# A perceiver layer on one core: chunks of 128 + 128 + 1 keys with the last key's products stacked, and layer norm vectors loaded as rows

## The chip, the cores and the metric

The kernel runs on one core of a Trainium2 chip. The core has a matrix engine (TensorE, PE in the rows), VectorE (DVE), ScalarE (ACT), GpSimd (POOL) and SyncE (SP), each with its own queue of instructions, and 16 DMA engines. The engines work side by side and wait for one another by semaphores. The metric is the device time of one execution in microseconds (us), as the median of several runs.

## The reference

Two layer norms, a cross attention over 257 keys for each of 32 batches, a self attention over 32 tokens, and a mixture of experts with two of eight experts for each token:

```python
x = x + xattn(layernorm(x), ctx, g_x, b_x, g_c, b_c, Wq, Wk, Wv, Wo)   # x (32, 32, 512), ctx (32, 257, 384)
x = x + attn(layernorm(x), W_qkv, W_o)
x = x + moe(layernorm(x), gate_w, gate_b, w1, b1, w2, b2, ln_g, ln_b)  # top 2 of 8, FF 2048

def xattn(x, context, ...):
    xn = layer_norm(x, g_x, b_x)
    cn = layer_norm(context, g_c, b_c)
    q, k, v = (heads(t) for t in (xn @ Wq, cn @ Wk, cn @ Wv))          # 16 heads of 64
    sim = einsum('bhid,bhjd->bhij', q, k) * 64 ** -0.5
    return merge(einsum('bhij,bhjd->bhid', softmax(sim), v)) @ Wo
```

## The kernel before

The 1024 tokens are eight groups of 128, and a group is four batches of 32 tokens. Groups 1 to 6 are one loop on each engine; groups 0 and 7 are written apart. The body of a group runs the cross attention of group g together with the self attention and the routing of group g - 1. After the groups comes the mixture of experts: 23 jobs of 128 rows, whose matmuls are lines 546 and 564.

The keys are not projected. The queries are carried through Wk into the 384 columns of the context (`qk_proj`, L1183), so the scores are products with the normalized context itself (`scores`, L1199), and so is the other side: `av` (L1240) multiplies the probabilities with the normalized context n. That product wants more than one half precision pass, so n and the probabilities p are each split into a high and a low half-precision part, and three products are summed in one PSUM bank: n_high·p_high, n_low·p_high and n_high·p_low.

The 257 keys of a batch stand on the partitions in three chunks, `PART = [86, 86, 85]` at `KOFF = [0, 86, 172]`. Each step per chunk is therefore done three times: the statistics of the context (`cn_stats`, L915 to L922), its normalization (`cn_apply`, L930), its high part (`n_hi`, ScalarE, L814) and low part (`n_lo`, VectorE, L969), the transposes of the context (`ct_fill`, L1208) and of the probabilities (`pt_fill`, L1222), the high part of those (`pt_hi`, ScalarE, L821), their low part (`pt_lo`, VectorE, L962), and the matmuls of `av`: three products of three chunks, nine for each 128 of the 384 columns (c = 0, 1, 2).

In a group, TensorE goes through steps b = 0 to 4. In step b stand the scores of batch b in four parts, with the transposes of the probabilities of batch b - 1 between (in step 0: the context transposes of batch 1), and then the three `av` of batch b - 1, in steps 1, 2 and 4 each with one `ct_fill` ahead for a batch to come. Step 1 also has the scores of the self attention (`ss_fill`, L1302), step 4 its product with the values (`pv_fill`, L1313). VectorE in step b reduces the scores of batch b, normalizes its probabilities (`norm_probs`, L955, for which `pt_fill` of step b + 1 waits), and normalizes a context ahead; in step 2 it also has `ss_sub` (L986, L987), after step 3 `ss_norm` (L993 to L999), for which `pv_fill` waits. The order on each engine is that of the code: `body` of each engine is written out by hand.

At the start, ScalarE loads the vectors g_x, b_x, g_c, b_c into columns (L771 to L774): one element to a partition, 1792 elements of 4 bytes. They are the scale and bias of `xn_out` (L782) and `ct_out` (L789). SyncE loads x, the weights and the contexts; each context is two transfers (`ctx_load`): 255 rows to 85 partitions, and the last two rows to partition 85. A context of the next group is loaded as soon as the third `av` of the batch in the same slot is done.

## Time and profile before

| | |
|---|---|
| median of 3 runs | 1579.29 us (1573.94 to 1582.66) |
| the profiled execution's own time | 1575.59 us |
| its span (first to last instruction) | 1574.0 us |
| mean granted TensorE clock | 0.981 |
| PE busy | 1472.5 us, 94% of the span |
| VectorE busy | 679.8 us, 43% |
| ScalarE busy | 448.8 us, 29% |
| GpSimd busy | 114.0 us, 7% |
| DMA | 140.25 MB, mean 89 GB/s |
| starts of the query matmuls of groups 2 and 3 | 221.33 and 317.55 us, 96.2 apart |

The span has three parts: until 24 us TensorE has next to nothing to do; from there to 850 us run the eight groups and the end of the routing; the jobs of the experts take the rest. Matmuls are pipelined, and the busy time of one (its mean of 0.38 us, say) is longer than the distance to the next: what a matmul costs a full TensorE is read from the starts of the rows.

### The profile page before, as it was taken

The numbers are of one execution on the slowest core, as the hardware profiler recorded it, in microseconds if no ns is written. First come the engines' busy times: TensorE is split into PE (matmuls) and PEld (weight loads), VectorE is DVE, ScalarE is ACT, GpSimd is POOL, SyncE is SP. The second block draws the span as 40 slices with busy tenths as digits, with TensorE's granted clock in tenths as the row PEclk, the third lists the DMA queues.
The fourth block names the chain that finished last, engine by engine and source line by source line (L and its number), as shares of the span: only waits on it lengthen the run. The fifth ranks groups of instructions, "written<-read, shape, count | busy, mean of one in ns | idle before, by whom it ended". The sixth has DMA issues, their size and how long they took to land.

```text
span 1574.0 us, 22638 instructions
## 1 busy us (share of the span) xinstructions
PE 1472.5 (94%) x7708; PEld 913.7 (58%) x7709; DVE 679.8 (43%) x1822; ACT 448.8 (29%) x916; POOL 114.0 (7%) x167
## 2 busy tenths in 40 slices
PE   3899999999999999999965999999999999999997
PEld 3668686686866769677552444444444444444442
DVE  2764747657476674765533312112112212212215
ACT  1553626445263452625401111111111111111100
POOL 1000010000100101010011000000000000000005
PEclk9999999999999999999976999999999999999997
DMA  8680000000000010000056251606051346000005
GB/s 276 229 303 2 31 24 10 30 13 30 23 18 22 13 32 22 20 23 12 1 214 236 105 225 68 240 13 260 20 214 59 121 152 260 14 19 20 13 7 167
DMA packets 42784, 140.25 MB, mean 89 GB/s; under 512 B 4792, under 2 KB 4792, under 8 KB 37632
## 3 DMA queue, kind: packets, MB, share of 16 engines
q0 software_dynamic: 16256, 83.89, 14.0%
q1 hardware_dynamic: 24640, 55.93, 10.5%
q8 instruction: 20, 0.33, 0.1%
q10 hardware_dynamic: 1856, 0.01, 0.1%
q14 instruction: 12, 0.10, 0.0%
HBM read 110.46 MB, written 29.36 MB: 89 GB/s over the span
## 4 chain that ended last, share of the span: by engine, by line
PE 80%; DVE 11%; issue 3%; ACT 2%; DMA 2%; POOL 1%; ACTq 0%; SPq 0%; DVEq 0%; POOLq 0%
PE bank L546 20%; PE bank L564 20%; PE bank L1199 7%; PE bank L1240 6%; PE bank L1162 4%; PE bank L1265 4%; PE bank L1183 3%; PE bank L1253 3%; PE bank L556 3%; PE bank L1287 2%; PE bank L1321 2%; PE bank L1222 2%; DMA ccol<-in_L_xattn_b_c_dram 1%; DVE mx L945 1%; DVE cstats L915 1%
## 5 line engine op out<-in xcount | busy, mean ns | idle before, releaser
L546 PE MATMUL bank<-moe_w,arena 128*128 x736 | 332.4, 595 | 2.3 <-POOL pool_mark L354 2.3
L564 PE MATMUL bank<-moe_w,arena 128*128 x736 | 330.9, 592 | 0.0
L458 DVE TENSOR_TENSOR arena<-bank,arena 128x512 f32<-128x512 f32 x92 | 63.7, 692 | 478.5 <-PE bank L546 478.5
L546 PEld LDWEIGHTS bank<-moe_w,arena 128*128 128x128 f32 x736 | 140.3, 191 | 178.7 <-issue 178.7
L396 ACT ACTIVATE arena<-arena 128x512 f32<-128x512 f32 x92 | 57.9, 630 | 578.6 <-DVE arena L458 578.6
L564 PEld LDWEIGHTS bank<-moe_w,arena 128*128 128x128 f32 x736 | 132.7, 190 | 132.5 <-issue 132.5
L1199 PE MATMUL bank<-moe_w 128*128 128x257 f32 x768 | 188.4, 382 | 2.4 <-DVE moe_w L765 2.4
L1240 PE MATMUL bank<-moe_w 86*128 86x512 f16 (+1 forms) x576 | 153.4, 379 | 5.1 <-ACT moe_w L821 3.3
L1199 PEld LDWEIGHTS bank<-moe_w 128*128 128x128 f32 x768 | 137.2, 190 | 21.8 <-DVE moe_w L765 2.6
L807 ACT ACTIVATE moe_w<-bank,ccol,ugain 128x512 f32<-128x512 f32 x96 | 74.6, 778 | 92.8 <-PE bank L1240 91.9
L962 DVE TENSOR_TENSOR moe_w<-bank,moe_w 86x512 f16<-86x512 f32 (+1 forms) x96 | 64.5, 685 | 69.7 <-ACT moe_w L821 69.5
L1240 PEld LDWEIGHTS bank<-moe_w 86*128 86x128 f16 (+1 forms) x576 | 54.0, 97 | 57.9 <-ACT moe_w L821 4.3
L1240 PE MATMUL bank<-moe_w,arena 86*128 86x512 f16 (+1 forms) x288 | 78.0, 379 | 0.0
L1162 PE MATMUL bank<-arena,moe_w 128*128 128x128 f32 x512 | 60.8, 281 | 13.4 <-ACT arena L782 13.4
L821 ACT CAST moe_w<-bank 86x512 f16<-86x512 f32 (+1 forms) x96 | 53.4, 580 | 54.6 <-PE bank L1222 54.6
L1162 PEld LDWEIGHTS bank<-arena,moe_w 128*128 128x128 f32 x512 | 59.7, 197 | 13.8 <-issue 13.8
L1222 PE MATMUL bank<-ident,moe_w 128*86 128x128 f32 (+1 forms) x384 | 55.5, 274 | 12.3 <-DVE moe_w L955 10.9
L556 PEld LDWEIGHTS bank<-ident,arena 128*128 128x128 f32 x368 | 45.3, 141 | 36.9 <-issue 36.9
L465 DVE COPY arena<-bank 128x512 f32<-128x512 f32 x92 | 62.9, 684 | 4.5 <-PE bank L556 2.9
L800 ACT ACTIVATE moe_w<-bank,negm 128x257 f32<-128x257 f32 x128 | 59.9, 473 | 10.0 <-DVE negm L947 9.5
L692 POOL TENSOR_TENSOR crstd<-cmv,half 86x3 f32<-86x3 f32 x32 | 30.1, 939 | 438.2 <-DVE cmv L922 438.2
L765 DVE COPY moe_w<-bank 128x512 f32<-128x512 f32 x48 | 33.1, 691 | 65.7 <-PE bank L1183 65.7
(188 smaller groups left out, 1595.4 us busy)
## 6 DMA issues: line engine op xcount, KB each, us to landing
moe_w<-in_L_ffn_w_dram POOLq DMA_DIRECT2D x16, 4096.0 KB, 19.4
xs_rows<-blocks SPq DMA_DIRECT2D x8, 2048.0 KB, 13.8
arena<-in_ctx_dram SPq DMA_DIRECT2D x32, 382.5 KB
arena<-in_L_ffn_b_dram POOLq DMA_DIRECT2D x8, 1024.0 KB, 26.7
arena<-xs_rows SPq DMA_DIRECT2D x23, 256.0 KB, 2.7
ys_rows<-arena SPq DMA_DIRECT2D x23, 256.0 KB, 2.0
moe_w<-in_L_xattn_Wq_dram SPq DMA_DIRECT2D x1, 2048.0 KB, 9.7
moe_w<-in_L_xattn_Wo_dram SPq DMA_DIRECT2D x1, 2048.0 KB, 21.8
```

What stands on the lines that cost most here:

```text
L458: nc.vector.tensor_tensor(h_sb[:, fb % 2, :], bank[fb % 2][:, :], b1_rows[:, bass.ds(slot * FF + fb * 512, 512)], ALU.add).then_inc(h_bias ...
L465: nc.vector.tensor_copy(hT_sb[:, fb % 2, :, :].rearrange("p c t -> p (c t)"), bank[2 + fb % 2][:, :]).then_inc(hT_out, 1)
L546: last = nc.tensor.matmul(bank[fb % 2][:, :], xsT[:, k, :], moe_flat[:, bass.ds((e % 2) * 16384 + k * FF + fb * 512, 512)], start=(k == 0) ...
L556: last = nc.tensor.transpose(bank[2 + fb % 2][:, c * P:(c + 1) * P], h_sb[:, fb % 2, c * P:(c + 1) * P], ident[:, :])
L564: last = nc.tensor.matmul(Y[:, :], hT_sb[:, fb % 2, c, :], moe_flat[:, bass.ds((e % 2) * 16384 + 8192 + (4 * fb + c) * DIM, DIM)], start=( ...
L807: nc.scalar.activation(uT[:, c, b, :, :], M[at % 2][:, :].rearrange("p (h t) -> p h t", t=TOK), ACT.Identity, bias=ccol[:, 1, c:c + 1], sc ...
L962: nc.vector.tensor_tensor(pT_low[0:PART[k], k, :], src[0:PART[k], :], pT_high[0:PART[k], k, :], ALU.subtract).then_inc(emptied, 1)
L1162: last = nc.tensor.matmul(ps[:, m * P:(m + 1) * P], wq[:, k, (4 * i + m) * P:(4 * i + m + 1) * P], xnT[:, k, :], start=(k == 0), stop=(k = ...
L1199: last = nc.tensor.matmul(bank[h][:, 0:KEYS], qkT[:, c, b, h * P:(h + 1) * P], cnT[:, b % 2, c, :], start=(c == 0), stop=(c == KC - 1))
L1222: last = nc.tensor.transpose(into[0:PART[k], h * P:(h + 1) * P], probs[:, h, KOFF[k]:KOFF[k] + PART[k]], ident[:, :])
L1240: last = nc.tensor.matmul(ps[:, :], n_part[0:PART[k], k, c * P:(c + 1) * P], p_part[0:PART[k], k, :], start=(k == 0 and i == 0), stop=(k = ...
L1265: last = nc.tensor.matmul(ps[:, 0:256], oT[:, m, :], wo[:, m, j * 256:(j + 1) * 256], start=(m == 0), stop=(m == KI - 1))
```

## The change

`PART` becomes [128, 128, 65] and `KOFF` [0, 128, 256]. The first 256 keys fill two chunks of 128 partitions. The last key stands three times in a third chunk of 65 partitions, in partitions 0, 32 and 64 (`LAST_AT`); the partitions between hold zeros, written once by GpSimd before the first context is loaded. For the last key the three products of `av` are stacked on those three partitions: partition 0 has n_high and p_high, partition 32 n_low and p_high (n_lo writes its third chunk there, into `n_high`), partition 64 n_high and p_low (pt_lo writes there, into `pT_high`). One matmul of 65 partitions sums the three, so `av` has 2 + 2 + 2 + 1 matmuls. The third transposes of the probabilities read the one column of the last key, broadcast to 65. A context is loaded by four transfers: 256 rows to 128 partitions, and the last row to each of three partitions.

The layer norm vectors are loaded as 14 rows of 128 elements into a free part of `y2`; one TensorE transpose turns them, ScalarE copies the 14 columns, and `gcol` and `ccol` are views of the copy.

```diff
@@ -46,8 +46,9 @@
 KI = INNER // P
 KF = FF // P
 HG = HEADS // GB
-PART = [86, 86, 85]
-KOFF = [0, 86, 172]
+PART = [P, P, 65]
+KOFF = [0, P, 2 * P]
+LAST_AT = (0, 32, 64)
 ZERO_FIRST = 3
 FB = FF // 512
 JOBS = TOKENS * TOPK // P + EXPERTS - 1
@@ -148,8 +149,10 @@
         before = sb("before", [P, P])
         ones = sb("ones", [P, P])
         gate = sb("gate", [P, KD, EXPERTS])
-        gcol = sb("gcol", [P, 2, KD])
-        ccol = sb("ccol", [P, 2, KC])
+        cols = sb("cols", [P, 2 * KD + 2 * KC])
+        gcol = cols[:, 0:2 * KD].rearrange("p (k c) -> p k c", k=2)
+        ccol = cols[:, 2 * KD:2 * KD + 2 * KC].rearrange("p (k c) -> p k c", k=2)
+        col_rows = y2[0:2 * KD + 2 * KC, 0:P]
         ugain = sb("ugain", [P, KC])
         gate_bias = sb("gate_bias", [P, EXPERTS])
         half = sb("half", [P, 8])
@@ -240,6 +243,7 @@
         x0_in = sem("x0_in")
         x_in, wk_in, wq_in, wv_in, wo_in = sem("x_in"), sem("wk_in"), sem("wq_in"), sem("wv_in"), sem("wo_in")
         qkv_in, wos_in, cols_in, rows_in, gate_in = sem("qkv_in"), sem("wos_in"), sem("cols_in"), sem("rows_in"), sem("gate_in")
+        cols_full, cols_ok = sem("cols_full"), sem("cols_ok")
         ctx_in = [sem(f"ctx_in{b}") for b in range(GB)]
         xs_zeroed = sem("xs_zeroed")
         consts, ident_ok, zeros_ok, memset_ok = sem("consts"), sem("ident_ok"), sem("zeros_ok"), sem("memset_ok")
@@ -251,7 +255,7 @@
         m_full, m_free = sem("m_full"), [sem(f"m_free{i}") for i in range(2)]
         qk_full, qk_out = sem("qk_full"), [sem(f"qk_out{i}") for i in range(2)]
         pt3_full, pt3_out = sem("pt3_full"), sem("pt3_out")
-        n_high_done, n_low_done, p_high_done, ugain_ok = sem("n_high_done"), sem("n_low_done"), sem("p_high_done"), sem("ugain_ok")
+        spare_zero, n_high_done, n_low_done, p_high_done, ugain_ok = sem("spare_zero"), sem("n_high_done"), sem("n_low_done"), sem("p_high_done"), sem("ugain_ok")
         b_full, b_free = sem("b_full"), sem("b_free")
         s_full, max_done, neg_done, exp_done = sem("s_full"), sem("max_done"), sem("neg_done"), sem("exp_done")
         rinv_done, norm_done = sem("rinv_done"), sem("norm_done")
@@ -617,10 +621,10 @@
         def ctx_load(sp, g, b):
 
             row = (g * GB + b) * KEYS
-            sp.dma_start(ctx[0:85, b, :, :].rearrange("p k c -> p (k c)"),
-                         ctx_rows[bass.ds(row, 255), :].rearrange("(p k) c -> p (k c)", k=3)).then_inc(ctx_in[b], 16)
-            sp.dma_start(ctx[85:86, b, 0:2, :].rearrange("p k c -> p (k c)"),
-                         ctx_rows[bass.ds(row + 255, 2), :].rearrange("(p k) c -> p (k c)", k=2)).then_inc(ctx_in[b], 16)
+            sp.dma_start(ctx[:, b, 0:2, :].rearrange("p k c -> p (k c)"),
+                         ctx_rows[bass.ds(row, 2 * P), :].rearrange("(p k) c -> p (k c)", k=2)).then_inc(ctx_in[b], 16)
+            for p in LAST_AT:
+                sp.dma_start(ctx[p:p + 1, b, 2, :], ctx_rows[bass.ds(row + 2 * P, 1), :]).then_inc(ctx_in[b], 16)
 
         @block.sync
         def _(sp):
@@ -632,6 +636,7 @@
 
             sp.dma_start(x_all[:, 0, :], x_rows[0:P, :]).then_inc(x0_in, 16)
             sp.dma_start(wq, Wq.rearrange("(c p) n -> p c n", p=P)).then_inc(wq_in, 16)
+            sp.wait_ge(spare_zero, 1)
             ctx_load(sp, 0, 0)
             sp.dma_start(wk_rows, Wk.rearrange("(c p) n -> p c n", p=P)).then_inc(wk_in, 16)
             sp.dma_start(qkv_rows, W_qkv.rearrange("(c p) n -> p c n", p=P)).then_inc(qkv_in, 16)
@@ -664,6 +669,7 @@
         def _(pool):
             nc.gpsimd.memset(ones[:, :], 1.0).then_inc(memset_ok, 1)
             nc.gpsimd.memset(half[:, :], -0.5).then_inc(memset_ok, 1)
+            nc.gpsimd.memset(ctx[:, :, 2, :], 0.0).then_inc(spare_zero, 1)
             pool.wait_ge(memset_ok, 2)
             nc.gpsimd.affine_select(out=ident[:, :], in_=ones[:, :], compare_op=ALU.is_equal, fill=0.0, base=0,
                                     pattern=[[-1, P]], channel_multiplier=1).then_inc(ident_ok, 1)
@@ -689,7 +695,7 @@
             def cn_pow(n):
 
                 pool.wait_ge(cn_var, n + 1)
-                nc.gpsimd.tensor_tensor(crstd[0:86, :], cmv[0:86, :, 1], half[0:86, 0:3], ALU.pow).then_inc(cn_rstd, 1)
+                nc.gpsimd.tensor_tensor(crstd[:, :], cmv[:, :, 1], half[:, 0:3], ALU.pow).then_inc(cn_rstd, 1)
 
             def body(g, do_a, do_b, nxt):
                 ln = ln_before(g)
@@ -767,12 +773,13 @@
 
         @block.scalar
         def _(act):
-            with nc.allow_non_contiguous_dma(reason="a few columns"):
-                act.dma_start(gcol[:, 0, :], g_x.rearrange("(c p) -> p c", p=P)).then_inc(cols_in, 16)
-                act.dma_start(gcol[:, 1, :], b_x.rearrange("(c p) -> p c", p=P)).then_inc(cols_in, 16)
-                act.dma_start(ccol[:, 0, :], g_c.rearrange("(c p) -> p c", p=P)).then_inc(cols_in, 16)
-                act.dma_start(ccol[:, 1, :], b_c.rearrange("(c p) -> p c", p=P)).then_inc(cols_in, 16)
-            act.wait_ge(cols_in, 64)
+            act.dma_start(col_rows[0:KD, :], g_x.rearrange("(c p) -> c p", p=P)).then_inc(cols_in, 16)
+            act.dma_start(col_rows[KD:2 * KD, :], b_x.rearrange("(c p) -> c p", p=P)).then_inc(cols_in, 16)
+            act.dma_start(col_rows[2 * KD:2 * KD + KC, :], g_c.rearrange("(c p) -> c p", p=P)).then_inc(cols_in, 16)
+            act.dma_start(col_rows[2 * KD + KC:, :], b_c.rearrange("(c p) -> c p", p=P)).then_inc(cols_in, 16)
+            act.wait_ge(cols_full, 1)
+            nc.scalar.copy(cols[:, :], BK[:, 0:2 * KD + 2 * KC]).then_inc(cols_ok, 1)
+            act.wait_ge(cols_ok, 1)
             nc.scalar.activation(ugain[:, :], ccol[:, 0, :], ACT.Identity, scale=1.0 / (N_SCALE * P_SCALE)).then_inc(ugain_ok, 1)
 
             def xn_out(n):
@@ -910,7 +917,7 @@
             def cn_stats(g, b):
 
                 bt, slot = GB * g + b, b % GB
-                dve.wait_ge(ctx_in[slot], 32 * (g + b // GB + 1))
+                dve.wait_ge(ctx_in[slot], 64 * (g + b // GB + 1))
                 for k in range(3):
                     last = nc.vector.bn_stats(cstats[0:PART[k], k, :], ctx[0:PART[k], slot, k, :])
                 link = chain(dve, cn_step, 2 * bt)
@@ -919,7 +926,7 @@
                 for k in range(3):
                     last = nc.vector.bn_aggr(cmv[0:PART[k], k, :], cstats[0:PART[k], k, :])
                 link(last)
-                nc.vector.tensor_scalar(cmv[0:86, :, 1], cmv[0:86, :, 1], EPS, None, ALU.add).then_inc(cn_var, 1)
+                nc.vector.tensor_scalar(cmv[:, :, 1], cmv[:, :, 1], EPS, None, ALU.add).then_inc(cn_var, 1)
 
             def cn_apply(g, b):
 
@@ -959,16 +966,16 @@
 
                 dve.wait_ge(p_high_done, 3 * (GB * g + b) + k + 1)
                 src, _, _, emptied = pt_place(g, b, k)
-                nc.vector.tensor_tensor(pT_low[0:PART[k], k, :], src[0:PART[k], :], pT_high[0:PART[k], k, :],
-                                        ALU.subtract).then_inc(emptied, 1)
+                rows, low = (slice(0, P), pT_low[:, k, :]) if k < 2 else (slice(64, 65), pT_high[64:65, 2, :])
+                nc.vector.tensor_tensor(low, src[rows, :], pT_high[rows, k, :], ALU.subtract).then_inc(emptied, 1)
 
             def n_lo(g, b):
 
                 dve.wait_ge(n_high_done, GB * g + b + 1)
                 for k in range(3):
-                    last = nc.vector.scalar_tensor_tensor(out=n_low[0:PART[k], b, k, :], in0=ctx[0:PART[k], b, k, :],
-                                                          scalar=N_SCALE, in1=n_high[0:PART[k], b % 2, k, :],
-                                                          op0=ALU.mult, op1=ALU.subtract)
+                    rows, low = (slice(0, P), n_low[:, b, k, :]) if k < 2 else (slice(32, 33), n_high[32:33, b % 2, 2, :])
+                    last = nc.vector.scalar_tensor_tensor(out=low, in0=ctx[rows, b, k, :], scalar=N_SCALE,
+                                                          in1=n_high[rows, b % 2, k, :], op0=ALU.mult, op1=ALU.subtract)
                 last.then_inc(n_low_done, 1)
 
             def heads_apart(g):
@@ -1219,7 +1226,8 @@
                 if k == 0:
                     pe.wait_ge(norm_done, GB * g + b + 1)
                 for h in range(HG):
-                    last = nc.tensor.transpose(into[0:PART[k], h * P:(h + 1) * P], probs[:, h, KOFF[k]:KOFF[k] + PART[k]], ident[:, :])
+                    part = probs[:, h, KOFF[k]:KOFF[k] + P] if k < 2 else probs[:, h, 2 * P:KEYS].to_broadcast([P, PART[2]])
+                    last = nc.tensor.transpose(into[0:PART[k], h * P:(h + 1) * P], part, ident[:, :])
                 last.then_inc(full, 1)
 
             def av(g, b, c):
@@ -1236,9 +1244,10 @@
                             pe.wait_ge(tp_free, tp(g, ("pt", b, 2)) + 1)
                         else:
                             pe.wait_ge(pt3_out, 2 * (g + 1))
-                    for k in range(3):
-                        last = nc.tensor.matmul(ps[:, :], n_part[0:PART[k], k, c * P:(c + 1) * P], p_part[0:PART[k], k, :],
-                                                start=(k == 0 and i == 0), stop=(k == 2 and i == 2))
+                    for k in range(2):
+                        nc.tensor.matmul(ps[:, :], n_part[:, k, c * P:(c + 1) * P], p_part[:, k, :], start=(k == 0 and i == 0), stop=False)
+                last = nc.tensor.matmul(ps[:, :], n_high[0:PART[2], b % 2, 2, c * P:(c + 1) * P], pT_high[0:PART[2], 2, :],
+                                        start=False, stop=True)
                 last.then_inc(m_full, 1)
 
             def o_proj(g, i):
@@ -1400,6 +1409,8 @@
                     rk_fill(g - 1)
 
             pe.wait_ge(ident_ok, 1)
+            pe.wait_ge(cols_in, 64)
+            nc.tensor.transpose(BK[:, 0:2 * KD + 2 * KC], col_rows, ident[0:2 * KD + 2 * KC, 0:2 * KD + 2 * KC]).then_inc(cols_full, 1)
             xn_fill(0, 2)
             pe.wait_ge(wq_in, 16)
             body(0, True, False, True)
```

The order of the instructions. First, TensorE in group 0, step 1: the last scores, and the first `ct_fill` and `av` (L1199, L1208 and L1240 before are L1206, L1215, and L1248 with L1249 now). A matmul of 32-bit data stands once here and twice in the trace. Before:

```order
L1199 MATMUL bank<-moe_w 128x257 x3
L1208 MATMUL bank<-ident,arena 128x86 x2
L1208 MATMUL bank<-ident,arena 128x85
L1240 MATMUL bank<-moe_w 128x512 x3
L1240 MATMUL bank<-moe_w,arena 128x512 x3
L1240 MATMUL bank<-moe_w 128x512 x3
```

With the change:

```order
L1206 MATMUL bank<-moe_w 128x257 x3
L1215 MATMUL bank<-ident,arena 128x128 x2
L1215 MATMUL bank<-ident,arena 128x65
L1248 MATMUL bank<-moe_w 128x512 x2
L1248 MATMUL bank<-moe_w,arena 128x512 x2
L1248 MATMUL bank<-moe_w 128x512 x2
L1249 MATMUL bank<-moe_w 128x512
```

Two of nine matmuls of 512 columns are gone, and the context transposes have 321 columns in place of 257. Next, the queue of ScalarE at the start; before:

```order
L771 DMA gcol<-in_L_xattn_g_x_dram 128x4x1
L772 DMA gcol<-in_L_xattn_b_x_dram 128x4x1
L773 DMA ccol<-in_L_xattn_g_c_dram 128x3x1
L774 DMA ccol<-in_L_xattn_b_c_dram 128x3x1
L776 ACT_TABLE_LOAD
L776 ACTIVATE ugain<-ccol 128x3 [waits cols_in]
L782 ACTIVATE arena<-bank,gcol 128x128 [waits tp_full]
```

With the change:

```order
L776 DMA arena<-in_L_xattn_g_x_dram 4x128
L777 DMA arena<-in_L_xattn_b_x_dram 4x128
L778 DMA arena<-in_L_xattn_g_c_dram 3x128
L779 DMA arena<-in_L_xattn_b_c_dram 3x128
L781 ACT_TABLE_LOAD
L781 COPY cols<-bank 128x14 [waits cols_full]
L783 ACTIVATE ugain<-cols 128x3 [waits cols_ok]
L789 ACTIVATE arena<-bank,cols 128x128 [waits tp_full]
```

The wait for the four transfers moves from ScalarE to TensorE, whose new first instruction (L1413) waits for them and for `ident`. Last, the queue of SyncE at the start; before:

```order
L634 DMA moe_w<-in_L_xattn_Wq_dram 128x4x1024
L620 DMA arena<-in_ctx_dram 85x1152
L622 DMA arena<-in_ctx_dram 1x768
L636 DMA moe_w<-in_L_xattn_Wk_dram 128x3x1024
L637 DMA moe_w<-in_L_attn_W_qkv_dram 128x4x512
```

With the change:

```order
L638 DMA moe_w<-in_L_xattn_Wq_dram 128x4x1024
L624 DMA arena<-in_ctx_dram 128x768
L627 DMA arena<-in_ctx_dram 1x384 x3
L641 DMA moe_w<-in_L_xattn_Wk_dram 128x3x1024
L642 DMA moe_w<-in_L_attn_W_qkv_dram 128x4x512
```

Each context has two more transfers to issue, and the first one now waits for GpSimd's zeros.

## Rows read from the trace of the kernel before

**Rows 1.** Windows: length, busy time of each engine, clock, DMA share, GB/s.

```profile
317.00:413.00 96.00, 92.28 (x708) 69.89 (x708) 62.80 (x188) 43.22 (x96) 8.41 (x12) 1.00 0.07 22
...
36.00:40.00 4.00, 2.53 (x24) 2.26 (x23) 1.03 (x3) 2.59 (x5) 0.00 (x0) 1.00 1.06 308
...
48.00:56.00 8.00, 7.18 (x66) 6.69 (x65) 4.77 (x12) 4.15 (x8) 0.55 (x1) 0.79 1.04 390
```

**Rows 2.** Timeline of the start: start, us, engine, line, tile [idle before].

```profile
2.23 1.79 POOL L682 MEMSET arena<- 128x2048 f32 x1
...
2.57 0.86 ACTq L774 DMA_DIRECT2D ccol<-in_L_xattn_b_c_dram  x1
...
9.55 1.09 PE L1273 MATMUL bank<-ident,arena 128*128 128x128 f32 x4 [9.55 <-DVE arena L900]
...
22.32 0.20 ACT L776 ACTIVATE ugain<-ccol 128x3 f32<-128x3 f32 x1 [17.58 <-DMA ccol<-in_L_xattn_b_c_dram]
...
24.07 9.19 PE L1162 MATMUL bank<-arena,moe_w 128*128 128x128 f32 x64 [13.43 <-ACT arena L782]
...
38.30 3.66 PE L1142 MATMUL bank<-ident,moe_w 128*128 128x128 f32 x32
...
47.06 5.47 PE L1183 MATMUL bank<-moe_w 64*128 64x128 f32 x64 [2.32 <-DVE moe_w L765]
```

**Rows 3.** Timelines of the start and of group 3: issues on SyncE's queue.

```profile
1.40 0.42 SPq L634 DMA_DIRECT2D moe_w<-in_L_xattn_Wq_dram  x1
...
4.17 4.00 SPq L638 DMA_DIRECT2D moe_w<-in_L_attn_W_o_dram  x1
...
358.55 0.26 SPq L620 DMA_DIRECT2D arena<-in_ctx_dram  x1
```

**Rows 4.** DMA issues: transfers, KB, median us from issue to landing.

```profile
moe_w<-in_L_xattn_Wq_dram SPq DMA_DIRECT2D x1, 2048.0 KB, 9.7
...
moe_w<-in_L_attn_W_o_dram SPq DMA_DIRECT2D x1, 1024.0 KB, 21.9
...
gcol<-in_L_xattn_b_x_dram ACTq DMA_DIRECT2D x1, 2.0 KB, 14.2
```

**Rows 5.** Timeline of TensorE in group 3.

```profile
350.72 0.81 PE L1240 MATMUL bank<-moe_w 86*128 86x512 f16 x3
...
352.67 0.39 PE L1208 MATMUL bank<-ident,arena 86*128 86x86 f32 x3
...
352.90 0.81 PE L1240 MATMUL bank<-moe_w 86*128 86x512 f16 x3
...
376.44 0.60 PE L1222 MATMUL bank<-ident,moe_w 128*85 128x128 f32 x4
...
384.27 1.51 PE L1222 MATMUL bank<-ident,moe_w 128*86 128x128 f32 x12
...
386.55 0.82 PE L1240 MATMUL bank<-moe_w 86*128 86x512 f16 x3 [0.55 <-ACT moe_w L821]
...
392.08 1.08 PE L1313 MATMUL bank<-blocks,v_sb 128*32 128x128 f32 x32 [1.22 <-DVE blocks L999]
```

**Rows 6.** Timeline of VectorE in group 3.

```profile
360.91 0.69 DVE L962 TENSOR_TENSOR moe_w<-bank,moe_w 86x512 f16<-86x512 f32 x1 [3.73 <-ACT moe_w L821]
...
367.32 1.47 DVE L915 BATCH_NORM_STATS2 cstats<-arena 86x6 f32<-86x384 f32 x3
...
375.51 0.69 DVE L962 TENSOR_TENSOR moe_w<-bank,moe_w 86x512 f16<-86x512 f32 x1 [2.40 <-ACT moe_w L821]
...
383.07 1.14 DVE L955 TENSOR_SCALAR moe_w<-moe_w,rinv 128x257 f32<-128x257 f32 x4
```

**Rows 7.** Timeline of ScalarE in group 3.

```profile
366.50 0.56 ACT L789 ACTIVATE moe_w<-bank,ccol 128x257 f32<-128x257 f32 x1
```

**Rows 8.** Timeline of VectorE in group 7.

```profile
759.67 0.69 DVE L962 TENSOR_TENSOR moe_w<-bank,moe_w 86x512 f16<-86x512 f32 x1 [4.87 <-ACT moe_w L821]
```

**Rows 9.** Waits of the first 135 us: total, times, longest.

```profile
DVE cstats L915 <- DMA arena<-in_ctx_dram: 12.6, 2, 7.0
```

## Prediction

> **What bounds the kernel now.** I read the windows first, for the share of TensorE by stage, then the timelines of TensorE, VectorE and ScalarE over one group beside one another, for which wait ends last, then the start, then the DMA issues. In group 3, as in every group of the loop, TensorE is busy 92.28 of 96 us at the full clock of 2.4 GHz [rows 1]. So a removed matmul could be worth its whole length, but only where no other engine stands right behind. Before 24.07 TensorE has only four transposes: ScalarE waits 17.58 us for the last of the column loads, and the query matmuls wait for ScalarE [rows 2]. The experts are untouched.
>
> **The start.** The column loads were issued by 3.4 us; the last lands at 22.3, and 1.75 us later the query matmuls begin (22.32 to 24.07) [rows 2]. That these loads are slow for their number of pieces and not their size I take from 2 KB that need 14.2 us [rows 4]. The new ones are 14 rows of 512 bytes. I take them to land before the transposes of x are done, at 9.55 + 1.09 = 10.64 [rows 2]. Then the next thing late is either Wq, issued at 1.40 and landed 9.7 later, at 11.1 [rows 3, 4], or ScalarE's part, 10.64 + 1.65 = 12.3 (the 1.75 without the 0.1 of `ugain`). So the query matmuls start at 12.3 in place of 24.07: -11.8. The new transpose and copy of 14 columns lie ahead of 10.64 and cost nothing; if the rows landed only at 14, each us behind 10.6 would be one less gained.
>
> GpSimd's zeros are 1,536 elements a partition; 2,048 take 1.79 [rows 2], so 1.34. That delays `ident` to about 3, unseen, and SyncE's first context by under 1 us, while the DMA engines still have Wq to do. Of the six extra issues of the first contexts each may hold the queue for a while. What is late next are the weights: the transposes of W_qkv and W_o would run at 38.30 - 11.8 = 26.5 [rows 2], and W_o lands at 4.17 + 21.9 = 26.1 [rows 3, 4]. That is no wait by 0.4. Bounds for the start: -8 (the weights land some 4 us later, through the extra issues) to -12.5 (ScalarE's 1.65 hidden in part).
>
> **Price of a matmul and a transpose.** From 350.72 to 352.67 stand the nine matmuls of an `av` (the row's three, three times): 1.95, so 0.217 each, and an `av` becomes 7 x 0.217 = 1.52, 0.43 less. From 352.67 to 352.90 a `ct_fill` takes 0.23 for 257 columns [rows 5]; for 321 by columns 0.29, +0.06. (Twelve transposes of 128 columns take 1.51 [rows 5], 0.126 each at most, which bounds it at +0.15.) Over 96 `av` that would be -41.7, over 96 `ct_fill` +5.8. ScalarE and VectorE have as many instructions of the same free size as before; rows of 85 and 86 partitions took the same in every group of the trace, so I take 0 for 128, 65 and 1. The broadcast weight load of 65 columns lies beside a matmul; I take 0, between -0.02 and +0.05 for each of 128.
>
> **A loop group, step by step** (times of before; in brackets the shift so far).
> - Step 0: three `ct_fill`, then VectorE's chain behind the last scores: [+0.18].
> - Step 1: three `av` save 1.30, three `ct_fill` cost 0.18. The second `ct_fill` must now wait for ScalarE's `ct_out`, which stands behind four exponentials (the same place in step 2: 366.50 + 0.56 [rows 7]): +0.2. VectorE has slack, since it sits idle 3.73 before 360.91 [rows 6]. [-0.8].
> - Step 2: the `av` get shorter, but the transposes at 376.44 [rows 5] wait for VectorE's instruction at 375.51 + 0.69 = 376.20 [rows 6], which by its chain (n_lo, statistics, norm_probs, apply, ss_sub, then ScalarE's exponential, n_hi, pt_hi) starts from step 2's last probabilities and not from an `av`. The slack is 0.1. [-0.9].
> - Step 3: `norm_probs` ends at 383.07 + 1.14 = 384.21, and the transposes that wait for it start at 384.27 [rows 5, 6]. No slack, and VectorE's own shift is still that of step 1: 1.3 saved turns into a wait. [-0.8].
> - Step 4: the first two `av` come before `pv_fill`, which already waits 1.22 for VectorE [rows 5]. Their 0.86 goes into that wait. The third saves 0.43, a `ct_fill` costs 0.06. [-1.2].
>
> So -1.2 in each of six groups: -7.2, of the 6 x (12 x 0.43 - 12 x 0.06) = 27 that the matmuls and transposes themselves give there. Bounds: -0.6 (the transposes at 0.15, more waits of step 1's kind) to -2.5.
>
> **Group 7** has no contexts ahead in steps 2 to 4. VectorE sits idle 4.87 in step 3 [rows 8], so steps 2 and 3 keep theirs: 0.18 - 1.0 - 0.9 - 1.3 - 0.4 = -3.5 (-2 to -4.5). **Group 0** has no `ss_sub`, so step 2 keeps 0.9: 0.18 - 0.9 - 0.9 and nothing in steps 3 and 4, in which VectorE waits for a context behind the filling of the expert rows (two waits on contexts, 12.6 in all, 7.0 of them at the start, so 5.6 here [rows 9]): -1.9 (-3 to +1, since all of it now comes 12 us closer to the same transfers).
>
> **The clock.** The changed groups leave TensorE idle 2.2 us ahead of `pv_fill` (1.22 + 0.86 and a little) and 1.6 us ahead of the transposes of step 4. In the trace an idle 2.32 before 47.06 [rows 2] was followed by a fall to 1.2 GHz: the window from 48 to 56 has a granted clock of 0.79, so 8 x 0.21 = 1.7 us lost [rows 1]. The shorter wait ahead of step 1's first transposes is in every loop group, at a full clock. I take one fall in the whole kernel, +1.7; bounds 0 to 7 x 1.7 = 12. The Trainium skill says in "TensorE: Matmul & The Clock Gate" (Part 4, PE-mode transpose) that transposes do not count as activity for the clock. By that rule the transposes and the waits ahead of and behind them in step 4 are one gap. Here 32 transposes followed others from 38.30 on, and the clock stayed at 1.00 [rows 1, 2], so the trace speaks against it. The gap would run from 382 to 386, 3.9 us, and cost a fall in each group; this is a rival below.
>
> **Sum.** -11.8 - 7.2 - 3.5 - 1.9 + 1.7 = -22.7. The profiled execution took 1575.6, so 1552.9; it lies 3.7 under the median of the runs, 1579.3, from which it would be 1556.6. Between the two I forecast 1554.
>
> **Rivals.**
> - *The clock falls once in each group* at `pv_fill` or by the gap of step 4: 12 in place of 1.7, 1564. For it: the one idle of this length in the groups was followed by a fall. Against it: that one had matmuls of 64 partitions only around it. 17%.
> - *It falls twice in each group*: 24, which takes all back: 1576, no change. 5%.
> - *The start gives little*, because rows or weights land late and the extra issues hold SyncE: half of it, 1560 to 1564. 10%.
> - *The removed matmuls count in full*: 1575.6 - 11.8 - 41.7 + 5.8 = 1528. For it: TensorE at 92.28 of 96. Against it: steps 2 to 4 above. 5%.
> - *The one-row transfers are slow*: a context is issued at 358.55 [rows 3], read at 367.32 [rows 6], 8.8 later. If a transfer of one row took the 14.2 of the 2 KB load [rows 4], VectorE would wait 5.4 in step 2, where there is no slack, in at least seven groups: 1553 + 38 = 1591 or more, slower. It decides from 8.8 us on. Against it: a transfer to one partition is part of each load now, and the loop shows no wait for it. 3%.
> - That the change does less than it says I see no room for: the matmuls are gone from the program. 2% for what I have not seen.
>
> **Chances.** My case 58%. A measurement of this kernel tells a change from none at about 0.5%, 7.9 us; faster by more are my case and all rivals but the twofold fall, the slow rows and part of the unseen: 0.91; within 0.5%: 0.06; slower: 0.03. The range holds my case with the bounds of its terms, and the first and third rival: 1545 to 1566; my case alone is 1547 to 1560.
>
> **What would show it.** Start: the first query matmul near 12.3, waiting for ScalarE, and the transposes of W_qkv without a wait. Loop: a period of 95.0 in place of 96.2; an `av` of 1.52 and a `ct_fill` of 0.29 by their starts; waits of some 1.6 and 2.2 us ahead of the transposes of step 4 (for VectorE's L955) and ahead of `pv_fill` (for its blocks), and about 0.8 at the third transposes of step 3. Wrong: a period under 94 (VectorE is no bound), a clock under 1.00 in a loop group, a wait for a context there, or a group 0 longer than before.

## The result, and the profile after

The changed kernel took 1566.57 us (median of 6 runs, 1562.93 to 1567.33), the kernel before 1579.3 us (1573.94 to 1582.66, 6 runs): a ratio of 0.9916, 95% interval 0.9901 to 0.9931. That is faster by 0.8%, by 12.7 us of the medians and by 9.0 us of the profiled spans (1574.0 to 1565.0). The forecast was 1554 with a range of 1545 to 1566: the direction was right, the gain too large by 10 to 14 us, and the time just outside the range.

By the starts of each group's query matmuls the two traces divide so:

| | before | after | difference | forecast |
|---|---|---|---|---|
| start of the query matmuls | 24.07 | 11.69 | -12.4 | -11.8 |
| group 0 | 101.15 | 99.5 | -1.6 | -1.9 |
| groups 1 to 6 | 6 x 96.2 | 585.2 | +8.0 | -7.2 and +1.7 for the clock |
| group 7 and the end of the routing | 148.3 | 145.2 | -3.1 | -3.5 |
| experts | 723.3 | 723.4 | +0.1 | 0 |

The start, from the timeline of TensorE and then of ScalarE after (it answers to [rows 2]):

```profile
7.03 0.25 PE L1413 MATMUL bank<-ident,arena 14*128 14x14 f32 x1 [7.03 <-DMA arena<-in_L_xattn_b_c_dram]
8.91 1.09 PE L1282 MATMUL bank<-ident,arena 128*128 128x128 f32 x4 [1.63 <-DVE arena L907]
11.69 9.36 PE L1169 MATMUL bank<-arena,moe_w 128*128 128x128 f32 x64 [1.69 <-ACT arena L789]
...
26.20 1.04 PE L1149 MATMUL bank<-ident,moe_w 128*128 128x128 f32 x8
```

```profile
10.04 1.51 ACT L789 ACTIVATE arena<-bank,cols 128x128 f32<-128x128 f32 x4 [2.31 <-PE bank L1282]
```

The fourteen rows are there at 7.03, ahead of the normed x. The transposes of the late weights (L1149) stand there without a wait, as forecast.

The loop did not get shorter. The three longest waits of TensorE in group 5 of the changed kernel (502 to 598 us): who waited for whom, total, times, longest.

```profile
PE bank L1230 <- DVE moe_w L962: 3.3, 2, 1.9
PE bank L1322 <- DVE blocks L1006: 2.1, 1, 2.1
PE bank L1230 <- DVE moe_w L970: 0.8, 1, 0.8
```

All three are for VectorE: L1230 are the transposes of the probabilities, L1322 is `pv_fill`. They are the waits that the prediction named: 1.9 ahead of the transposes of step 4 (forecast 1.6), 2.1 ahead of `pv_fill` (2.2) and 0.8 in step 3 (0.8); the other 1.4 of the first line was there before. Windows of the changed kernel (columns as in [rows 1]): groups 2 and 5; then group 2 during `pv_fill`, which follows the wait of 2.09, and in the four us behind it; then the transposes of step 4 in group 3.

```profile
209.00:307.00 98.00, 90.44 (x686) 68.64 (x685) 64.00 (x189) 43.08 (x96) 8.61 (x12) 0.98 0.07 22
...
502.00:598.00 96.00, 88.43 (x683) 67.76 (x683) 63.87 (x188) 43.08 (x96) 8.41 (x12) 1.00 0.07 22
284.00:285.00 1.00, 0.89 (x32) 0.84 (x32) 1.00 (x3) 0.00 (x0) 0.00 (x0) 1.00 0.00 0
285.00:289.00 4.00, 4.00 (x19) 1.85 (x12) 2.92 (x14) 1.41 (x3) 0.85 (x1) 0.57 0.01 2
374.00:378.00 4.00, 3.82 (x18) 3.21 (x19) 3.16 (x6) 2.28 (x4) 0.00 (x0) 0.57 0.17 69
```

TensorE's busy time in a group went from 92.28 [rows 1] to 88.43 where the clock stays up, 3.9 us less, and the group takes no less: 97.9, 98.0, 97.0, 97.9, 96.3 and 98.0 us for groups 1 to 6, against 96.2. VectorE, on which TensorE waits, has gone up from 62.80 [rows 1] to 63.87. In four groups the granted clock falls to the lower level (1.2 GHz) behind `pv_fill`, in a fifth at the transposes of step 4; only group 5 has none. The timelines of TensorE in groups 2 and 5 show what a fall costs:

```profile
284.11 1.08 PE L1322 MATMUL bank<-blocks,v_sb 128*32 128x128 f32 x32 [2.09 <-DVE blocks L1006]
...
285.46 1.02 PE L1248 MATMUL bank<-moe_w 128*128 128x512 f16 x2
286.27 1.06 PE L1248 MATMUL bank<-moe_w,arena 128*128 128x512 f16 x2
```

```profile
577.10 1.08 PE L1322 MATMUL bank<-blocks,v_sb 128*32 128x128 f32 x32 [2.09 <-DVE blocks L1006]
...
578.45 0.59 PE L1248 MATMUL bank<-moe_w 128*128 128x512 f16 x2
578.88 0.59 PE L1248 MATMUL bank<-moe_w,arena 128*128 128x512 f16 x2
```

Two f16 matmuls of 512 columns take 0.81 by their starts (285.46 to 286.27) instead of 0.43. A group with such a fall is 1.5 to 1.7 us longer than group 5, the one with the fall at step 4 0.7 (97.0). The wait is 2.09 in both cases, so its length alone does not decide.

Group 5 had no fall and was still 1.3 longer than the forecast of 95.0. VectorE in group 3 (timeline):

```profile
353.22 0.69 DVE L970 TENSOR_TENSOR moe_w<-bank,moe_w 1x512 f16<-1x512 f32 x1 [0.53 <-ACT moe_w L828]
353.94 0.42 DVE L952 TENSOR_REDUCE mx<-bank 128x1 f32<-128x257 f32 x1
...
355.03 1.01 DVE L977 SCALAR_TENSOR_TENSOR arena<-arena,moe_w 128x384 f16<-128x384 f32 x2
356.06 0.55 DVE L977 SCALAR_TENSOR_TENSOR moe_w<-arena,moe_w 1x384 f16<-1x384 f32 x1
356.64 1.48 DVE L922 BATCH_NORM_STATS2 cstats<-arena 128x6 f32<-128x384 f32 x3
...
364.85 0.69 DVE L970 TENSOR_TENSOR moe_w<-bank,moe_w 128x512 f16<-128x512 f32 x1 [2.40 <-ACT moe_w L828]
365.46 0.41 DVE L952 TENSOR_REDUCE mx<-bank 128x1 f32<-128x257 f32 x1
```

From the low part of 128 partitions to the next instruction are 0.61 us (364.85 to 365.46), from that of one partition 0.72 (353.22 to 353.94). The three low parts of a context take 1.61 (355.03 to 356.64). In the kernel before these were:

```profile
338.00 1.48 DVE L969 SCALAR_TENSOR_TENSOR arena<-arena,moe_w 86x384 f16<-86x384 f32 x3
339.40 0.41 DVE L945 TENSOR_REDUCE mx<-bank 128x1 f32<-128x257 f32 x1
```

that is, 1.40. The duration of each instruction is as before; what has grown is the distance to its neighbours: 0.1 from the probabilities' low part to the instruction behind it, and 0.2 for the context's.

In steps 3 and 4 the probabilities' instruction follows another one of VectorE without a wait for ScalarE, and there it also starts late itself. The three low parts of the probabilities in step 4, of the changed kernel (group 5) and of a kernel whose low parts all start on partition 0 (`low_scratch`, below; group 3), by VectorE's timelines:

```profile
570.33 2.01 DVE L970 TENSOR_TENSOR moe_w<-bank,moe_w 128x512 f16<-128x512 f32 x3 [0.20 <-ACT moe_w L828]
572.37 0.69 DVE L1000 TENSOR_REDUCE ssum<-sS 128x16 f32<-128x512 f32 x1
```

```profile
368.29 1.88 DVE L970 TENSOR_TENSOR moe_w<-bank,moe_w 128x512 f16<-128x512 f32 x3 [0.21 <-ACT moe_w L828]
370.09 0.67 DVE L1000 TENSOR_REDUCE ssum<-sS 128x16 f32<-128x512 f32 x1
```

That is 2.04 against 1.80. Not all of it reaches the path: laid beside each other instruction by instruction, the two groups show that the 0.2 of the first two contexts go into waits for TensorE and ScalarE, and that the probabilities' four (0.14, 0.12, 0.20, 0.24) and the last two contexts' (0.22, 0.23) add up to the 1.15 by which VectorE is late at `blocks`, and the group with it.

### The profile page after: what moved, and what is told of

It is laid out like the page before. It is cut to its first block, busy times and chain, and to the rows that moved or that the text cites. A ratio compares the mean times of both kernels' runs of the same rounds, so it can differ in the third digit from the quotient of the medians.

```text
span 1565.0 us, 22371 instructions
## 1 busy us (share of the span) xinstructions
PE 1449.6 (93%) x7517; PEld 901.9 (58%) x7518; DVE 689.5 (44%) x1822; ACT 448.3 (29%) x917; POOL 115.2 (7%) x168
## 4 chain that ended last, share of the span: by engine, by line
PE 79%; DVE 13%; issue 4%; ACT 2%; POOL 2%; DMA 1%; DVEq 0%; ACTq 0%; SPq 0%; POOLq 0%
PE bank L550 20%; PE bank L568 20%; PE bank L1206 8%; PE bank L1169 4%; PE bank L1274 4%; PE bank L1248 3%; PE bank L1190 3%; PE bank L1262 3%; PE bank L560 3%; PE bank L1296 2%; PE bank L1230 2%; PE bank L1330 2%; DVE mx L952 2%; DVE cstats L922 1%; PE bank L1215 1%
## 5 line engine op out<-in xcount | busy, mean ns | idle before, releaser
L1206 PE MATMUL bank<-moe_w 128*128 128x257 f32 x768 | 188.7, 383 | 2.4 <-DVE moe_w L771 2.4
L1206 PEld LDWEIGHTS bank<-moe_w 128*128 128x128 f32 x768 | 137.3, 190 | 21.6 <-DVE moe_w L771 2.6
L1248 PE MATMUL bank<-moe_w 128*128 128x512 f16 x384 | 117.7, 389 | 4.6 <-ACT moe_w L828 2.5
L814 ACT ACTIVATE moe_w<-bank,cols,ugain 128x512 f32<-128x512 f32 x96 | 74.5, 777 | 64.8 <-PE bank L1249 64.8
L970 DVE TENSOR_TENSOR moe_w<-bank,moe_w 128x512 f16<-128x512 f32 (+1 forms) x96 | 65.6, 690 | 58.2 <-ACT moe_w L828 57.5
L1230 PE MATMUL bank<-ident,moe_w 128*128 128x128 f32 (+1 forms) x384 | 57.2, 279 | 29.5 <-DVE moe_w L962 23.9
L828 ACT CAST moe_w<-bank 128x512 f16<-128x512 f32 (+1 forms) x96 | 53.7, 582 | 66.8 <-PE bank L1230 66.8
L1230 PEld LDWEIGHTS bank<-ident,moe_w 128*128 128x128 f32 (+1 forms) x384 | 45.8, 141 | 45.3 <-DVE moe_w L962 26.9
L796 ACT ACTIVATE moe_w<-bank,cols 128x257 f32<-128x257 f32 x96 | 54.2, 564 | 25.4 <-PE bank L1215 25.2
L698 POOL TENSOR_TENSOR crstd<-cmv,half 128x3 f32<-128x3 f32 x32 | 30.1, 940 | 425.8 <-DVE cmv L929 425.8
## 6 DMA issues: line engine op xcount, KB each, us to landing
xs_rows<-blocks SPq DMA_DIRECT2D x8, 2048.0 KB, 12.4
```

Source lines behind the costliest of these rows:

```text
L814: nc.scalar.activation(uT[:, c, b, :, :], M[at % 2][:, :].rearrange("p (h t) -> p h t", t=TOK), ACT.Identity, bias=ccol[:, 1, c:c + 1], sc ...
L970: nc.vector.tensor_tensor(low, src[rows, :], pT_high[rows, k, :], ALU.subtract).then_inc(emptied, 1)
L1206: last = nc.tensor.matmul(bank[h][:, 0:KEYS], qkT[:, c, b, h * P:(h + 1) * P], cnT[:, b % 2, c, :], start=(c == 0), stop=(c == KC - 1))
L1230: last = nc.tensor.transpose(into[0:PART[k], h * P:(h + 1) * P], part, ident[:, :])
L1248: nc.tensor.matmul(ps[:, :], n_part[:, k, c * P:(c + 1) * P], p_part[:, k, :], start=(k == 0 and i == 0), stop=False)
```

## The experiments

All were timed in five rounds beside the kernel before, whose median was 1576.8 to 1577.2 us there and 1579.3 beside the changed kernel, which was not timed again: so up to 2.5 us of a difference of medians to the changed kernel can be that, and the ratios are the safer comparison. Periods are the distances between the query matmuls of groups 1 to 7. Periods and falls are those of one profiled execution of each kernel; the others differ in span and mean clock, so their falls may differ too. The four of `from0` below, for example, have spans of 1551.3 (the profiled one) to 1557.2 us at mean clocks of 0.980 to 0.977.

**Which half gave the gain?** The kernel before with the layer norm rows alone (all four loads, the transpose and the copy):

```diff
-                act.dma_start(gcol[:, 0, :], g_x.rearrange("(c p) -> p c", p=P)).then_inc(cols_in, 16)
...
+            act.dma_start(col_rows[0:KD, :], g_x.rearrange("(c p) -> c p", p=P)).then_inc(cols_in, 16)
...
```

> The kernel before with the vectors loaded as rows and turned by one transpose, and the keys still in chunks of 86, 86 and 85. By the traces the query matmuls of group 0 start 12.4 us earlier in the changed kernel; if all of that belongs to this part and nothing gives it back, 1579 - 12.4 = 1567, with a loop group of 96.2 as before. If part of the start's gain came from the new context transfers, less than 10 us.

Measured: 1564.34 us, ratio 0.992 (0.9899 to 0.994), span 1561.3; query matmuls at 11.51, six periods of 96.2. The rows alone give all of the gain, 12.5 us against the kernel before beside them, where 12.4 were expected; on top of them the chunks gave nothing.

**The chunks alone**, with the four old column loads and without their transpose and copy:

```diff
-            act.dma_start(col_rows[0:KD, :], g_x.rearrange("(c p) -> c p", p=P)).then_inc(cols_in, 16)
...
+                act.dma_start(gcol[:, 0, :], g_x.rearrange("(c p) -> p c", p=P)).then_inc(cols_in, 16)
...
```

> The changed kernel with the old column loads: chunks of 128, 128 and 1, the last key stacked. Theory (clock and VectorE): a loop group is 96.3 us where the clock stays up and 98.0 where it falls after the wait ahead of the product of the self attention's probabilities and values, so the kernel is 2 to 5 us slower than before, 1581 to 1584. The prediction's sum for this part alone was -10.9, so 1568.

Measured: 1573.69 us, ratio 0.9981 (0.9968 to 0.9994), span 1571.4. This is neither the 1581 to 1584 of my theory nor the prediction's 1568. The periods are 96.2, 96.9, 98.0, 96.3, 98.0 and 97.0: falls of both kinds, in five groups; that of the first, at step 4, costs nothing, since the wait ahead of `pv_fill` is shorter by it (1.13). The start was 4.4 us earlier than before, which I had not seen coming; by ScalarE's timeline of this kernel the last of the old loads had landed at 17.92, where it was 22.32 before [rows 2]:

```profile
17.92 0.20 ACT L779 ACTIVATE ugain<-ccol 128x3 f32<-128x3 f32 x1 [13.51 <-DMA ccol<-in_L_xattn_b_c_dram]
```

So the same column loads took 4.4 us less in this execution than in that of the kernel before; whether the other transfers did that is not shown. The loop of this kernel lost 5.3 us against before, which the start and groups 0 and 7 gave back.

**Is it the clock?** Two 32-bit matmuls of 512 columns, whose result nobody reads, fill the wait ahead of `pv_fill`:

```diff
                         if do_b and b == GB and c == 1:
+                            if do_a:
+                                filler()
                             pv_fill(g - 1)
+                for k in range(2):
+                    nc.tensor.matmul(bank[1][:, :], ident[:, :], wq[:, k, 0:512], start=True, stop=True)
```

> The changed kernel with two more 32-bit matmuls of 512 columns (0.86 us each) into a free bank just ahead of that product, where TensorE waits 2.09 us for VectorE. They compute nothing that is used. If the fall of the clock to 1.2 GHz after this wait costs 1.7 us in five of six groups: a clock of 1.00 in every loop group, periods of 96.3, and 7 to 9 us less than the changed kernel, 1558 to 1560. If the fall comes from something else (the wait ahead of the last transposes, the load of the engine over a longer time), or costs nothing: 1566, or later by up to 12 if the matmuls end up on the path.

Measured: 1561.01 us, ratio 0.9897 (0.9878 to 0.9915); periods 97.0, 96.3, 96.8, 96.3, 96.3, 96.3. Timeline of TensorE in group 2, where the changed kernel had its fall:

```profile
279.89 1.88 PE L1235 MATMUL bank<-moe_w,ident 128*128 128x512 f32 x4
282.14 1.08 PE L1326 MATMUL bank<-blocks,v_sb 128*32 128x128 f32 x32 [0.37 <-DVE blocks L1006]
...
283.49 0.59 PE L1252 MATMUL bank<-moe_w 128*128 128x512 f16 x2
283.92 0.59 PE L1252 MATMUL bank<-moe_w,arena 128*128 128x512 f16 x2
```

The work lies in the wait (0.37 us are left of 2.09) and every fall behind `pv_fill` is gone: 5.6 us less for doing more, where 7 to 9 were expected. By the ratios it is 3 us, and their intervals overlap; what shows the clock as a cause is the same filling on the kernel with 32 partitions below, timed beside it. What is left are two groups of 96.8 and 97.0, falls at step 4 (0.71 of the clock from 370 to 374 us in the windows of group 3), and a fall-free group of 96.3, so that something else is a cause too.

**Is it VectorE's instructions on one partition?** Both are written on 65 partitions into scratch instead. This leaves the low parts of the last key out (its high product is summed three times):

```diff
-(slice(64, 65), pT_high[64:65, 2, :])
+(slice(0, 65), pT_low[0:65, 2, :])
-(slice(32, 33), n_high[32:33, b % 2, 2, :])
+(slice(0, 65), n_low[0:65, b, 2, :])
```

> The changed kernel, but VectorE's two instructions on the last key's chunk work on 65 partitions and write to the low parts' own tiles and not on one partition into the high parts' tiles. It leaves the low parts of the last key out (its high product is summed three times). If an instruction on one partition cannot lie over its neighbours as the others do: the next instruction starts 0.61 us after pt_lo's third and not 0.72, n_lo's three take 1.40 and not 1.61, VectorE's chain is 0.3 us shorter in each step, a group without a fall is 95.0 to 95.5, and the kernel 5 to 8 us shorter than the changed one. If those instructions cost the same on one partition: no change, 1566.

Measured: 1553.2 us, ratio 0.9846 (0.9825 to 0.9866); periods 96.7, 95.2, 95.2, 96.8, 95.2, 95.2. Timeline of VectorE:

```profile
333.22 0.69 DVE L970 TENSOR_TENSOR moe_w<-bank,moe_w 65x512 f16<-65x512 f32 x1 [0.53 <-ACT moe_w L828]
333.83 0.41 DVE L952 TENSOR_REDUCE mx<-bank 128x1 f32<-128x257 f32 x1
...
334.90 1.48 DVE L977 SCALAR_TENSOR_TENSOR arena<-arena,moe_w 128x384 f16<-128x384 f32 x3
336.30 1.47 DVE L922 BATCH_NORM_STATS2 cstats<-arena 128x6 f32<-128x384 f32 x3
```

The spacings are 0.61 and 1.40 again, and a group without a fall takes 95.2, nearly the forecast 95.0. So these eight instructions cost 1.1 us of every group. Against the changed kernel it is 13 us (11 by the ratios) and not the 5 to 8 expected; its profiled execution also had two falls instead of five. But "one partition" and "another start partition" had changed together.

**Few partitions, or their place?** The same products on 32 partitions each: the probabilities' low part from 32, the context's from 0.

```diff
-(slice(64, 65), pT_high[64:65, 2, :])
+(slice(32, 64), pT_high[32:64, 2, :])
-(slice(32, 33), n_high[32:33, b % 2, 2, :])
+(slice(0, 32), n_high[0:32, b % 2, 2, :])
```

> The changed kernel, with the same products stacked, but with the low part of the last key's probabilities written on partitions 32 to 63 (its product stands on 32) and the low part of its context row on partitions 0 to 31 (its product stands on 0); the high product is on partition 64. VectorE's two instructions so have 32 partitions instead of one, everything else is as in the changed kernel. Theory A (an instruction on one partition takes VectorE longer than one on many): the next instruction starts 0.61 us after the third low part of the probabilities (0.72 in the changed kernel) and 1.40 us after the three low parts of a context began (1.61); a group without a clock fall takes 95.2 us, one or two of six have a fall of 1.6: about 1553 us, as with scratch on 65 partitions. Rival B (what counts is that the instruction writes in place, or starts on another partition than 0): the spacings stay 0.72 for the probabilities, which start on 32, and at most the contexts' are repaired: 1559 to 1563. Rival C (it grows as the partitions get fewer, 32 is between): 1558 to 1562 with both spacings halfway.

Measured: 1560.85 us, ratio 0.9892 (0.9876 to 0.9908); periods 97.4, 95.9, 95.9, 97.5, 95.9, 95.9. My theory A fell and rival B came true, in time and in spacings. VectorE in group 3 (timeline):

```profile
335.90 0.68 DVE L970 TENSOR_TENSOR moe_w<-bank,moe_w 32x512 f16<-32x512 f32 x1 [0.53 <-ACT moe_w L828]
336.62 0.42 DVE L952 TENSOR_REDUCE mx<-bank 128x1 f32<-128x257 f32 x1
...
337.71 1.02 DVE L977 SCALAR_TENSOR_TENSOR arena<-arena,moe_w 128x384 f16<-128x384 f32 x2
338.64 0.54 DVE L977 SCALAR_TENSOR_TENSOR moe_w<-arena,moe_w 32x384 f16<-32x384 f32 x1
339.11 1.46 DVE L922 BATCH_NORM_STATS2 cstats<-arena 128x6 f32<-128x384 f32 x3
```

Thirty-two partitions from 32 on are followed by the same 0.72 as one partition was; thirty-two from 0 on need 0.47, and the three together 1.40.

**One partition, but the first:**

```diff
-(slice(64, 65), pT_high[64:65, 2, :])
+(slice(0, 1), pT_high[0:1, 2, :])
```

> The changed kernel with one edit: the low part of the last key's probabilities is written on partition 0 instead of 64 (its product then stands on 0, the high product on 64). It is still an instruction on one partition. Theory A' (VectorE loses time not where an instruction has few partitions, but where it starts on another partition than 0; the 32 partitions from 32 cost 0.71 us to the next instruction, those from 0 cost 0.47): the next instruction starts 0.61 us after this one, the context's low part, still on partition 32, keeps its 0.58 and the three together 1.61; a group without a fall takes 95.7 us, with falls in two to five of six: 1558 to 1563 us. Rival (one partition is slow wherever it is, and 32 from partition 32 are slow for another reason): 0.72 us as before, 96.3 a group, 1565 to 1567 us.

Measured: 1554.66 us, ratio 0.9854 (0.9835 to 0.9873); periods 97.1, then five of 95.6. Timeline of VectorE:

```profile
334.63 0.68 DVE L970 TENSOR_TENSOR moe_w<-bank,moe_w 1x512 f16<-1x512 f32 x1 [0.53 <-ACT moe_w L828]
335.24 0.40 DVE L952 TENSOR_REDUCE mx<-bank 128x1 f32<-128x257 f32 x1
```

One partition is no slower than 128 where it is partition 0: 0.61. The time is 3 us below my range, since only one group had a fall. Moving one slice from 64 to 0 goes with 12 us less (10 by the ratios). Of them the spacings explain 0.75 in each of six groups (96.3 to 95.6), some 4.5; most of the rest are falls that did not come in this execution, and why they did not is not shown.

**Both from partition 0, with the full result.** The high product needs a partition where neither factor is low, so the probabilities' instruction covers all 65 and a column of zeros and minus ones decides where the low part comes:

```diff
-                nc.vector.tensor_tensor(low, src[rows, :], pT_high[rows, k, :], ALU.subtract).then_inc(emptied, 1)
+                    nc.vector.scalar_tensor_tensor(out=high, in0=high, scalar=keep[0:PART[2], 0:1], in1=src[0:PART[2], :],
+                                                   op0=ALU.mult, op1=ALU.add).then_inc(emptied, 1)
```

> The changed kernel with both low parts of the last key written by instructions that start on partition 0, with the full result: the context's on partitions 0 to 31; the probabilities' on partitions 0 to 64, as the high part times a column (minus one on partitions 32 to 63, zero on the others) plus the whole value, so that partition 32 gets the low part and 0 and 64 the high one. Theory A': spacings of 0.61 and 1.40 us as with the scratch, a group without a fall takes 95.2 us, two of six have one: 1552 to 1555 us. Rival (an instruction with three sources here takes longer, or scratch on its own is what helped): 95.8 a group or more, 1558 to 1562 us.

Measured: 1555.21 us, ratio 0.9863 (0.9839 to 0.9887); periods 95.3 and five of 95.4, and no fall. The profiled execution is the fastest of the four; the slowest is 5.9 us longer at a lower mean clock, so it may well have had falls. The instruction itself is a little dearer: 0.66 to the next, by VectorE's timeline.

```profile
333.42 0.74 DVE L977 SCALAR_TENSOR_TENSOR moe_w<-moe_w,keep,bank 65x512 f16<-65x512 f16 x1 [0.53 <-ACT moe_w L829]
334.08 0.41 DVE L956 TENSOR_REDUCE mx<-bank 128x1 f32<-128x257 f32 x1
```

**The kernel with 32 partitions and the filled wait.** Its edit is the two diffs shown above, of the 32 partitions and of `filler`, together.

> As the kernel with 32 partitions, with two unused 32-bit matmuls of 512 columns ahead of the product with the values, in the wait of about 2 us. Theory A (the rest of the falls is from that wait): no fall in any group, 95.2 us each: 1551 to 1552 us. Rival (falls come from the wait ahead of step 4's transposes): one or two stay, 1553 to 1554 us. If the matmuls reach out of the wait: 1556 us or more.

Measured: 1556.19 us, ratio 0.9862 (0.9844 to 0.9881); all six periods 95.8 or 95.9. The filling took both falls away, and 4.7 us: the slowest execution with it (1557.64) is faster than the fastest without (1559.39). The 1551 to 1552 expected rested on 95.2 a group; the level of 95.8 is that of the probabilities' instruction from partition 32, and the filling does not reach out of the wait, of which 0.37 is left.

**VectorE's queue in another order**, on the kernel with 32 partitions. `norm_probs` of step 3 goes ahead of the statistics, their use behind `ss_norm`; ScalarE's exponential comes in step 3 instead of 2:

```diff
-                    if ahead:
+                    if ahead and b < 3:
                         cn_stats(g, b + 2)
                     if do_a:
                         norm_probs(g, b)
+                    if ahead and b == 3:
+                        cn_stats(g, b + 2)
...
                     ss_norm(g - 1)
                 if nxt:
+                    cn_apply(g, 5)
                     cn_stats(g, 6)
```

> As the kernel with 32 partitions, and a new order in step 3 and 4: VectorE scales the probabilities of context 3 before the statistics of the next group's second context (0.9 us of work moved behind it) and applies these statistics behind the softmax of the self attention; ScalarE's exponentials of the self attention come one step later. Theory A (the wait of 1.9 us ahead of step 4's transposes and that of 1.8 to 2.1 us ahead of the product with the values are VectorE's queue): both get shorter by about 1 us each or go, and so does every fall of the clock: a group takes 93.2 to 94.5 us, the whole 1540 to 1548 us. Rival (the time then is bounded by ScalarE or by VectorE's sum of work over the group, and the waits come back elsewhere): 95 us a group, 1550 to 1553.

Measured: 1554.77 us, ratio 0.9858 (0.984 to 0.9877), above both expected ranges (1540 to 1548, 1550 to 1553); periods 93.8, then five of 95.5 or 95.6. TensorE in group 3 of this kernel:

```profile
370.40 1.08 PE L1325 MATMUL bank<-blocks,v_sb 128*32 128x128 f32 x32 [2.09 <-DVE blocks L1006]
...
372.00 1.06 PE L1251 MATMUL bank<-moe_w 128*128 128x512 f16 x2
```

The order is worth about 2 us a group (93.8 without a fall, 95.9 with the old order), but the fall now came in five of six groups and took 1.8 of them back. The wait of 2.09 stayed, against theory A.

**The same order without the chunks** (the kernel before with the rows and this order):

> The kernel before with only the layer norm vectors as rows, and with the new order of VectorE's and ScalarE's steps 3 and 4 (the keys in chunks of 86, 86 and 85, nothing stacked). It tells whether the chunks are worth anything once VectorE's queue is out of the way. Theory A (the chunks take 1.2 us of TensorE's path off a group, which VectorE's waits took back): this one takes 95.0 to 95.7 us a group, 1557 to 1561 us, 8 us or more above the same order with the chunks. Rival (the chunks never stood on the path): equal to the same order with the chunks within 3 us.

Measured: 1568.66 us, ratio 0.9944 (0.9928 to 0.9959); periods 96.6 or 96.7, half a us more than with the old order. The expected 95.0 to 95.7 did not come. The one wait that is longer than with the old order, by TensorE's waits of group 3 (0.5 there):

```profile
PE bank L1247 <- ACT moe_w L825: 1.3, 1, 1.3
```

The waits for VectorE (1.4 and 1.2 us) are as long as with the old order, so there was nothing for the new one to shorten, and ScalarE's later exponential was only a cost. The kernel is 14 us above the same order with the chunks; 4 of these are what the order costs here. Against the best kernel without chunks, the rows alone with 1564.34, the chunks with this order are worth 10 us.

**All together:** both low parts from partition 0, the order, the filled wait.

> As the kernel with both low parts from partition 0, with the new order of VectorE's and ScalarE's steps 3 and 4 and with the two unused 32-bit matmuls ahead of the product with the values. The same order with the probabilities from partition 32 and no unused matmuls took 95.5 us a group, with a wait of 2.1 us ahead of that product and the clock at half speed behind it in every group. Theory A (the fall costs 1.6 us in each group, the start partition 0.6): 93.3 us a group, 1539 to 1544 us. Rival (the wait ahead of that product grows by what is saved elsewhere, since VectorE's queue is the bound of the step): 94.5 us or more, 1547 to 1552 us.

Measured: 1540.52 us (5 runs, 1539.12 to 1541.15), ratio 0.9761 (0.9742 to 0.9779), with the full result: the fastest, 26 us under the changed kernel (24 by the ratios) and as theory A had it. Periods 93.5, then five of 93.6. TensorE's waits in group 3:

```profile
PE bank L1241 <- DVE moe_w L966: 1.4, 1, 1.4
PE bank L1263 <- ACT moe_w L829: 1.2, 1, 1.2
...
PE bank L1337 <- DVE blocks L1014: 0.2, 1, 0.2
```

## Why the prediction was right in part and wrong in size

*The start* held: 11.69 for 12.3. The next thing late was ScalarE's part, TensorE did not wait for the weights, and the rows had landed by 7.0, far ahead of 10.6.

*The price of a matmul and a transpose* held: 1.52 for an `av` (367.39 to 368.91) and 0.28 for a `ct_fill` (379.02 to 379.30). So did the mechanism that most of it turns into waits for VectorE in steps 2 to 4; 27 us of matmuls went, and the fall-free group of the scratch kernel is 95.2 for the 95.0 forecast. TensorE's timeline in group 3 of the changed kernel:

```profile
367.39 0.59 PE L1248 MATMUL bank<-moe_w 128*128 128x512 f16 x2
...
368.91 0.59 PE L1248 MATMUL bank<-moe_w 128*128 128x512 f16 x2
...
379.02 0.44 PE L1215 MATMUL bank<-ident,arena 128*128 128x128 f32 x3
379.30 0.60 PE L1248 MATMUL bank<-moe_w 128*128 128x512 f16 x2
```

*"ScalarE and VectorE have as many instructions of the same free size [...] so I take 0 for 128, 65 and 1"* failed for VectorE. The term is +1.1 us a group, 0 taken: 6.6 us in groups 1 to 6, and 7.8 with the 0.2 a group by which even 95.2 missed. I had looked at how long an instruction is by its free size and not at whether it may overlap its neighbours. The new low parts start on partitions 64 and 32 and everything around them on 0. In the runs, partition 64 (one row), 32 (one row) and 32 (32 rows) each cost 0.1 us at the instruction behind, and 0 (one, 32 or 65 rows) nothing; with no wait ahead of it such an instruction also starts 0.1 late itself (the context's: 1.03 for the two before it, 0.93 in the kernel with 32 partitions). And since VectorE had no slack in steps 2 and 3, as the forecast itself said, it went on the path.

The Trainium skill states this in "VectorE: DVE Perf Modes", section "Two Vector instructions with no wait between them": an instruction whose input or output starts in another group of 32 partitions than the last one read or written in that memory is held until all earlier ones have finished; how many partitions it has does not come into it. Every spacing shown here agrees. The page gives no price; the 0.1 and 0.2 are these traces'. By that rule, looked up beforehand, the term would have had its sign.

*"I take one fall in the whole kernel, +1.7; bounds 0 to 7 x 1.7 = 12"* failed too: five came in the loop, 4 x 1.7 + 0.7 = 7.5 us. A clock under 1.00 in a loop group was one of the prediction's own signs of being wrong. The rival "the clock falls once in each group", 1564 at 17%, had the right mechanism for this part, but that its time comes so near is partly luck: it counted 12 us of falls where 7.5 came, and nothing for VectorE, which cost as much again. I had argued against it from where the one known fall stood; the row itself, 2.32 idle and a fall, was the better guide, though not a sure one (see below). Its variant by the Trainium skill's rule on transposes ("TensorE: Matmul & The Clock Gate", Part 4) did not hold as the cause: of six groups with the same transposes in step 4 only one fell there. Both misses, (7.5 - 1.7) + 7.8 = 13.6, are the gap between the forecast for groups 1 to 6, -5.5, and the +8.0 that came.

*Groups 0 and 7* have slips of addition in the forecast: its own terms give 0.18 - 0.9 - 0.9 = -1.6 and not -1.9, and -3.4 and not -3.5, so its sum would be -22.3 and not -22.7. Measured were -1.6 and -3.1.

**Open:** why a wait of 2.09 us is followed by a fall in one group and not in the next. I found nothing in the rows ahead of the wait that tells them apart, and a second place says the same: the wait of 2.3 us behind the first 32 of the start's L1183 matmuls (`qk_proj`; it ends at 47.06 in the kernel before [rows 2], at 34 to 42 us in the others) stands in all thirteen kernels of this document, behind and ahead of the same matmuls. In the profiled executions the clock fell behind it in seven kernels, the one before and the changed one among them, and not in the other six. So whether a fall comes is not settled by the length of the wait and its neighbours. Of the eleven kernels in which it ends between 34 and 36 us, the five where it ends first (34.37 to 34.96) had the fall, the six others (35.11 to 35.72) did not; and the kernel with the new order fell in five groups alike, 95.5 us apart, but not in its first. Both speak for when the wait comes and not for what is in it, but it can be chance: no run shifted a wait on purpose. The kernel with both low parts from 0 waits 2.0 us ahead of `pv_fill` in all six groups and had no fall in the execution that was profiled, where the changed kernel had four; that is no proof that the one is safe and the other not. Nor was it tried why the old column loads landed 4.4 us earlier in one kernel.

## What to carry to other kernels

Before removing work from the busiest engine, follow the queue of the engine that it waits for; there an instruction that starts on another partition than its neighbours costs more than its duration shows. A removed piece of work that turns into a wait can cost more than it saved, where the clock falls behind the wait; unused matmuls in it got 4.7 us back. When falls of the clock are counted, one profiled execution is not enough: look at the spread of the runs too. A few columns of a vector are loaded as rows and turned.

## What the runs showed that I had not expected

- A VectorE instruction from partition 32 or 64 between ones from 0: +0.1 us to the next, +0.2 where it also follows one without a wait; from 0, on 1, 32 or 65 partitions, nothing.
- Waits of 2.09 and of 2.3 us on TensorE with and without a fall behind them, and a fall after 1.89. A fall cost 1.7 us of a group in front of f16 matmuls of 512 columns, 0.7 at step 4.
- Column loads of 1.5 and 2 KB in pieces of 4 bytes: the last had landed at 22.32 in the kernel before and at 17.92 in another; as rows of 512 bytes they were there by 7.03.
